# Row-tiled attention masks, and the row maxima sent out from two DMA queues

## Chip, core and metric

The kernel runs on one core of one Trainium2 chip. The metric is the device time in microseconds (us) of one execution. Engines: TensorE (PE; its weight loads PEld), VectorE (DVE), ScalarE (ACT), GpSimd (POOL), and SyncE (SP), which issues most DMAs.

## The reference

A gated block: cross attention of 32 batches (128 queries, 128 keys, 16 heads of 8 dimensions), then a gated mixture of 8 experts on the 4096 tokens.

```
q, k, v = heads(layernorm(x) @ Wq.T + bq), heads(ctx @ Wk.T + bk), heads(ctx @ Wv.T + bv)
scores = einsum('bhqd,bhkd->bhqk', q, k) / sqrt(8)
scores = where(mask[:, None], finfo.min, scores)            # mask: (32, 128, 128) bool
out = merge(softmax(scores) @ v) @ Wo.T + bo
x = x + tanh(g_xattn) * out
w = adapted gate of layernorm(x) over 8 experts, h_e = gelu(y @ W1_e + b1_e)
x = x + tanh(g_ffn) * sum_e w_e * (h_e @ W2_e + b2_e)
```

## The kernel before

**Two phases.** The attention phase walks 16 groups (`g`) of two batches (`b`). Every engine runs `body(it)` for `it` from -6 to 19; `group_at(it, n)` is the group `it + n` if there is one, so that one iteration holds steps of several groups: inputs transposed three ahead, keys and queries (`kq`) two ahead, scores of group `it`, and normalization, Wo and the second layer norm of groups behind. The order of each engine's work is written out by hand, and semaphores tie them. The feed-forward phase (`body_b`) follows, with blocks of 512 tokens; some of its first matmuls are laid into the last attention iterations.

**Scores twice.** `natural(g, b)` makes scores with queries on the partitions: 16 matmuls of 24 rows, four row groups beside each other, into four banks. Then masks are added by matmuls that accumulate: the diagonal matrix `masked_ident` (-2^126) times the mask. Banks 2 and 3 (the low part) come first, banks 0 and 1 (`natural_rest`) later. VectorE takes the negated row maxima out of each pair (`maxima`, L719), splits them into a high and a low part (`max_split`), TensorE transposes the 32 rows (16 high, 16 low; L1147 for b = 0, "max0", and L1215 for b = 1, "max1"), ScalarE copies them to `maxT` (L645, L595), and SP sends them by two DMAs (L415, L407: high parts to row 24 of each row group, low parts to row 25) into `kq_st`. `transposed(g, b)` then makes the scores with keys on the partitions and the maxima taken off (26 rows), with masks again, and ScalarE takes exp (L559) in two halves of two banks. `values` multiplies by v, and `headsT` is copied out, transposed back and normalized to `merged`, which goes through a transpose, a ScalarE copy (`mergedT`, L602) and Wo (L1114).

**Orders that matter here.** On TensorE one iteration is: max1 of the group before, natural(g, 0), transposes of merged and x2n, natural_rest, Wo, values(g-1, 0), kq, transposed(g-1, 1), max0, transposed_rest(g-1, 1), inputs, natural(g, 1), values(g-1, 1), natural_rest(g, 1), v, transposed(g, 0) with its rest, gate, heads. On ScalarE: maxT of max1, exp(g-1, 0, rest), mergedT, x2T, headsT, kq, maxT of max0, exp(g-1, 1, low), exp(g-1, 1, rest), headsT, inputs, exp(g, 0, low). natural(g, 1) waits for exp(g-1, 1, low), since they share banks 2 and 3. On SP: max1's DMAs, then x, ctx, FFN weights and mask (`inputs_ahead`), the four stacks of 192 KB (`stacks`), max0's DMAs, and the stores of kq (`stores`).

**Idle turns** (L972) are matmuls without use at the start, which fill TensorE's waits.

## Time and profile before

| | |
|---|---|
| median of 3 runs | 627.77 us (626.75 to 628.27) |
| profiled execution, whole | 625.05 us |
| its span | 623.2 us |
| busy: PE, DVE, ACT, POOL | 95%, 77%, 61%, 29% |
| instructions | 13765 |

The span runs from the first to the last instruction of the profiled execution. A busy share is an average over both phases. A duration of a matmul in a timeline holds its way through the array, so matmuls overlap; the distance from one start to the next is what it costs.

### The profile page before, as it was taken

The page shows a single profiled execution, that of the slowest core. Times are in us where ns is not written, and L with a number is a line of the kernel's source. Part 1 is how long each engine was busy: PE and PEld are TensorE (multiplying, and loading weights), DVE is VectorE, ACT ScalarE, POOL GpSimd, SP SyncE. Part 2 cuts the span into 40 slices and gives each one's busy share as a digit, 9 for nine tenths or more (in the row PEclk, how much of TensorE's full clock was granted, in tenths as well). Part 3 has the DMA queues.
Part 4 walks back from the last instruction along what each step waited for, and adds up shares of the span by engine and source line. Part 5 has one row for each costly group of instructions (what it writes and reads, how often), then busy time and mean ns, then how long its engine had stood idle before and what let it go on. Part 6 is the DMA issues. An engine that isn't in the chain of part 4 may idle for free.

```text
span 623.2 us, 13765 instructions
## 1 busy us (share of the span) xinstructions
PE 593.8 (95%) x4490; PEld 452.0 (73%) x4490; DVE 479.4 (77%) x940; ACT 378.6 (61%) x625; POOL 178.9 (29%) x224
## 2 busy tenths in 40 slices
PE   7699899999999998999999999999999999999998
PEld 6556566666666655788878788787887887887886
DVE  3457677777776776578879788888888888888886
ACT  2134455555555545767777677677677676776673
POOL 7523344444444221212113212212112112121121
PEclk9969899999999999999999999999999999999999
DMA  6854556555655520041121121111121121111210
GB/s 183 223 150 129 153 160 175 142 141 151 172 150 152 160 64 5 3 102 44 44 68 35 56 68 52 50 57 44 50 67 50 34 67 50 50 61 40 67 51 17
DMA packets 43998, 55.12 MB, mean 88 GB/s; under 512 B 9520, under 2 KB 27824, under 8 KB 42416
## 3 DMA queue, kind: packets, MB, share of 16 engines
q1 hardware_dynamic: 43504, 53.99, 30.5%
q8 instruction: 29, 0.48, 0.3%
q10 hardware_dynamic: 448, 0.53, 0.2%
q14 instruction: 17, 0.14, 0.1%
HBM read 39.16 MB, written 14.81 MB: 87 GB/s over the span
## 4 chain that ended last, share of the span: by engine, by line
PE 82%; DMA 6%; ACT 4%; SPq 4%; DVE 2%; issue 2%; ACTq 0%; DVEq 0%
PE ps_h L1059 10%; PE ps_h L1061 9%; PE ps_h L1060 9%; PE ps_y L1074 9%; PE ps_y L1076 9%; PE ps_y L1075 9%; PE misc L1037 4%; DMA kq_st<-maxT 4%; PE scores L975 4%; PE scores L1003 3%; PE scores L1015 3%; PE scores L992 2%; ACT probs L559 2%; PE misc L1114 1%; DMA kq_scratch<-kq_parts 1%
## 5 line engine op out<-in xcount | busy, mean ns | idle before, releaser
L583 ACT ACTIVATE h_sb<-ps_h,b_sb 128x512 f32<-128x512 f32 x256 | 176.1, 690 | 102.1 <-PE ps_h L1061 92.1
L742 DVE TENSOR_TENSOR h_low<-h_sb,h_high 128x512 fp32r<-128x512 f32 x256 | 164.5, 682 | 0.1
L522 POOL TENSOR_TENSOR yT<-yT,weighted 128x512 f32<-128x512 f32 x54 | 70.9, 1313 | 277.9 <-DVE weighted L917 277.9
L738 DVE CAST h_high<-h_sb 128x512 fp32r<-128x512 f32 x128 | 97.7, 763 | 52.9 <-ACT h_sb L583 52.7
L719 DVE TENSOR_REDUCE neg_max<-scores 128x8 f32<-128x1024 f32 x64 | 77.9, 1221 | 49.1 <-PE scores L975 49.1
L1059 PE MATMUL ps_h<-x_high,w_high 128*128 (+1 forms) x256 | 101.9, 398 | 2.1 <-ACT h_sb L583 2.0
L1074 PE MATMUL ps_y<-h_high,w_high 128*128 128x512 f32 x256 | 100.2, 391 | 0.3 <-ACT h_high L587 0.3
L1061 PE MATMUL ps_h<-x_high,w_low 128*128 (+1 forms) x256 | 99.8, 390 | 0.0
L1076 PE MATMUL ps_y<-h_high,w_low 128*128 128x512 f32 x256 | 99.7, 389 | 0.0
L1060 PE MATMUL ps_h<-x_low,w_high 128*128 (+1 forms) x256 | 99.7, 389 | 0.0
L1075 PE MATMUL ps_y<-h_low,w_high 128*128 128x512 f32 x256 | 99.6, 389 | 0.0
L587 ACT ACTIVATE h_high<-ps_h,b_sb 128x512 fp32r<-128x512 f32 x128 | 87.3, 682 | 0.0
L559 ACT ACTIVATE probs<-scores 128x1024 f32<-128x1024 f32 x64 | 62.9, 1006 | 17.8 <-PE scores L1003 17.8
L1059 PEld LDWEIGHTS ps_h<-x_high,w_high 128*128 128x128 f32 x256 | 48.1, 188 | 14.5 <-issue 4.7
L1074 PEld LDWEIGHTS ps_y<-h_high,w_high 128*128 128x128 f32 x256 | 48.0, 188 | 11.2 <-ACT h_high L587 0.7
L1061 PEld LDWEIGHTS ps_h<-x_high,w_low 128*128 128x128 f32 x256 | 48.1, 188 | 10.3
L1076 PEld LDWEIGHTS ps_y<-h_high,w_low 128*128 128x128 f32 x256 | 48.0, 188 | 10.2
L1075 PEld LDWEIGHTS ps_y<-h_low,w_high 128*128 128x128 f32 x256 | 48.1, 188 | 9.9
L1060 PEld LDWEIGHTS ps_h<-x_low,w_high 128*128 128x128 f32 x256 | 48.1, 188 | 9.3
L917 DVE SCALAR_TENSOR_TENSOR weighted<-ps_y,b_sb,w_row 128x512 f32<-128x512 f32 x55 | 41.0, 745 | 0.0
L975 PE MATMUL scores<-mask_b,masked_ident 128*128 128x512 bf16 x128 | 40.2, 402 | 0.0
L1037 PE MATMUL misc<-probs,v_pad 128*32 128x128 f32 x1024 | 36.3, 285 | 0.3 <-issue 0.3
(127 smaller groups left out, 720.9 us busy)
## 6 DMA issues: line engine op xcount, KB each, us to landing
w_row<-w_scratch SPq DMA_DIRECT2D x64, 256.0 KB, 3.1
kq_st<-kq_scratch SPq DMA_DIRECT2D x64, 192.0 KB
kq_scratch<-kq_parts SPq DMA_DIRECT2D x30, 256.0 KB, 3.2
w_raw<-in_w_ffn SPq DMA_DIRECT2D x16, 256.0 KB, 3.7
kq_scratch<-kq_parts SPq DMA_DIRECT2D x32, 128.0 KB, 3.3
ctx_sb<-in_ctx SPq DMA_DIRECT2D x16, 128.0 KB, 2.6
out_y<-y_out SPq DMA_DIRECT2D x7, 256.0 KB, 2.3
x_all<-in_x SPq DMA_DIRECT2D x13, 128.0 KB, 2.2
```

The lines of the kernel that those rows point to most:

```text
L559: nc.scalar.activation(probs[:, b, half * 8 * S:(half + 1) * 8 * S], scores[:, 2 + 2 * half:4 + 2 * half, :].rearrange("p r x -> p (r x)") ...
L583: nc.scalar.activation(h_sb[:, j % HBUF, :], ps_h[:, j % 4, :], ACT.Gelu_apprx_tanh, bias=b1_sb[:, j:j + 1]).then_inc(h_done, 1)
L587: nc.scalar.activation(h_high[:, j % HBUF, :], ps_h[:, j % 4, :], ACT.Gelu_apprx_tanh, bias=b1_sb[:, j:j + 1]).then_inc(high_even, 1)
L719: nc.vector.tensor_reduce(neg_max[:, b, rows, :], scores[:, rows, :].rearrange("p r (s k) -> p r s k", k=S), AX.X, ALU.max, negate=True).t ...
L738: nc.vector.tensor_copy(h_high[:, j % HBUF, :], h_sb[:, j % HBUF, :]).then_inc(high_odd, 1)
L742: nc.vector.tensor_tensor(h_low[:, j % HBUF, :], h_sb[:, j % HBUF, :], h_high[:, j % HBUF, :].bitcast(F32), ALU.subtract).then_inc(low2_do ...
L1059: mm(dst, w_high[:, e, cols], xh, start=True, stop=False)
L1060: mm(dst, w_high[:, e, cols], xl, start=False, stop=False)
L1061: mm(dst, w_low[:, e, cols], xh, start=False, stop=True).then_inc(h_full, 1)
L1074: mm(dst, w_high[:, E + e, cols], h_high[:, j % HBUF, :], start=(f == 0), stop=False)
L1075: mm(dst, w_high[:, E + e, cols], h_low[:, j % HBUF, :], start=False, stop=False)
L1076: mm(dst, w_low[:, E + e, cols], h_high[:, j % HBUF, :], start=False, stop=(f == FC - 1)).then_inc(w2_done, 1)
```

## The change

Masks: each group's mask is loaded once per batch and repeated for the four row groups (rows 32r to 32r+31 hold queries 4i to 4i+3 in four slices `j`), 128 KB a group instead of 32 KB, by two DMAs, into one buffer instead of two; POOL converts 1024 elements a partition instead of 256. A mask of one pair of banks is 8 matmuls of 32 rows: natural ones of 32x32 with 512 columns, transposed ones of 32x128 with 128 columns. Query columns are dealt out in the order 4i+j when xn is transposed, and put back in the headsT copies. SP: max0's and max1's DMA carries the high parts alone, and the low parts are issued by ScalarE right behind its own copy, ahead of its next exp; masks and ctx stay ahead of the stacks, weights and x move behind max0's DMA, and the six later weights to the end of iteration 0. `merged`, `mergedT` and `x2n` have one buffer instead of two. Three idle turns are new ahead of transposed(0, 0), and six instead of two stand ahead of the first max0.

```diff
-        mask_words = sa("mask_words", [P, 2, GB, S // 4], I32)
-        mask_b = sa("mask_b", [P, 2, GB, S], BF16)
+        mask_words = sa("mask_words", [P, GB, S], I32)
+        mask_b = sa("mask_b", [P, 2, GB, 4, S], BF16)
...
+            def load_mask(g):
+                for b in range(GB):
+                    every = bass.AP(a["mask"].tensor, (g * GB + b) * 32 * S, [[0, ROWS], [S, 32], [1, S]])
+                    sp.dma_start(mask_words[:, b, :], every).then_inc(mask_in[g % 2], 16)
...
+            def masks_and_contexts(it):
+                if (g := group_at(it, 1)) is not None:
+                    if g > 0:
+                        sp.wait_ge(mask_done, g)
+                        load_mask(g)
...
-                    for n in range(2):
-                        sp.dma_start(kq_st[24 + n::32, g % 3, :, 1, 1 * S:(1 + 1) * S].bitcast(F32), maxT[n * H:(n + 1) * H, 1, :].bitcast(F32)).then_inc(max_in[1][g % 3], 16)
+                    sp.dma_start(kq_st[24::32, g % 3, :, 1, 1 * S:(1 + 1) * S].bitcast(F32), maxT[0:H, 1, :].bitcast(F32)).then_inc(max_in[1][g % 3], 16)
                 if it != -1:
-                    inputs_ahead(it)
+                    masks_and_contexts(it)
                 stacks(it)
                 if (g := group_at(it, 0)) is not None:
                     misc_wait_read(sp, "max0", g)
...
+                if it != -1:
+                    weights_and_x(it)
                 stores(it)
                 if it == -1:
-                    inputs_ahead(it)
+                    masks_and_contexts(it)
+                    weights_and_x(it)
+                elif it == 0:
+                    later_weights()
...
                     nc.scalar.activation(maxT[:, 1, :], misc[0:2 * H, bank_of("max1"), 0:S], ACT.Copy).then_inc(misc_read[bank_of("max1")], 1)
+                    misc_wait_read(act, "max1", g)
+                    wait_count(act, tr_low_full, 2 * (g - 3) + 2)
+                    nc.scalar.dma_start(kq_st[25::32, g % 3, :, 1, 1 * S:(1 + 1) * S].bitcast(F32), maxT[H:2 * H, 1, :].bitcast(F32)).then_inc(max_in[1][g % 3], 16)
                     exps(g, 0, 1)
...
-            def natural_mask(r, b, u):
-                return mm(scores[:, r, :].rearrange("p (s k) -> p s k", s=SLABS), masked_ident[:],
-                          mask_b[:, u, b, :].unsqueeze(1).to_broadcast([P, SLABS, S]), start=False, stop=True)
+            def natural_mask(pair, b, u):
+                for j in range(4):
+                    for r in pair:
+                        rows = slice(32 * r, 32 * r + 32)
+                        ins = mm(scores[32 * j:32 * j + 32, r, :].rearrange("p (s k) -> p s k", s=SLABS), masked_ident[rows, rows],
+                                 mask_b[rows, u, b, j, :].unsqueeze(1).to_broadcast([32, SLABS, S]), start=False, stop=True)
+                return ins
...
+            def transposed_mask(pair, b, u):
+                for j in range(4):
+                    for r in pair:
+                        rows = slice(32 * r, 32 * r + 32)
+                        ins = mm(scores[:, 2 + r, :].rearrange("p (s j i) -> p j s i", s=SLABS, j=4)[:, j], mask_b[rows, u, b, j, :],
+                                 masked_ident[rows, rows].unsqueeze(1).to_broadcast([32, SLABS, 32]), start=False, stop=(j == 3))
+                return ins
...
             def transposed(g, b, u):
+                if g == 0 and b == 0:
+                    idle_turns(3)
...
                     if g == 0:
-                        idle_turns(2)
+                        idle_turns(6)
                     pe.wait_ge(max_done[0], g + 1)
```

## Rows read from the trace of the kernel before

**Rows 1.** The page: TensorE's granted clock in tenths, 40 slices.
```profile
PEclk9969899999999999999999999999999999999999
```

**Rows 2.** Timeline of one iteration, TensorE: start us, us, engine, line.
```profile
139.26 0.61 PE L975 MATMUL scores<-mask_b,masked_ident 128*128 128x512 bf16 x2
...
139.70 0.39 PE L966 MATMUL misc<-ident_sb,merged 128*128 128x128 f32 x2
...
140.65 0.68 PE L1114 MATMUL misc<-wo_sb,mergedT 128*128 128x128 f32 x4
...
145.85 0.67 PE L992 MATMUL scores<-kq_st 24*128 24x128 f32 x16 [0.28 <-ACT probs L559]
...
146.45 0.60 PE L975 MATMUL scores<-mask_b,masked_ident 128*128 128x512 bf16 x2
...
146.98 1.08 PE L1037 MATMUL misc<-probs,v_pad 128*32 128x128 f32 x32
...
148.00 0.61 PE L975 MATMUL scores<-mask_b,masked_ident 128*128 128x512 bf16 x2
...
151.11 0.58 PE L1194 MATMUL misc<-wg_sb,x2T_sb 128*128 128x9 f32 x4
```

**Rows 3.** Timeline of the same iteration, the other engines.
```profile
138.73 0.27 ACT L595 ACTIVATE maxT<-misc 32x128 fp32r<-32x128 f32 x1 [0.38 <-PE misc L1215]
...
139.03 1.19 SPq L407 DMA_DIRECT2D kq_st<-maxT  x2
...
140.12 0.39 ACT L602 ACTIVATE mergedT<-misc 128x256 f32<-128x256 f32 x1 [0.22 <-PE misc L966]
...
144.53 0.27 ACT L645 ACTIVATE maxT<-misc 32x128 fp32r<-32x128 f32 x1 [0.40 <-PE misc L1147]
144.71 1.90 ACT L559 ACTIVATE probs<-scores 128x1024 f32<-128x1024 f32 x2
...
147.00 0.40 POOL L505 CAST mask_b<-mask_words 128x256 bf16<-128x256 uint8 x1
...
148.64 1.23 DVE L719 TENSOR_REDUCE neg_max<-scores 128x8 f32<-128x1024 f32 x1 [0.33 <-PE scores L975]
...
150.27 0.70 DVE L853 TENSOR_TENSOR v_pad<-misc,bv_row 128x128 f32<-128x128 f32 x2
```

**Rows 4.** Timeline of ScalarE at the start: its DMA issues and what follows.
```profile
12.69 0.61 ACTq L553 DMA_DIRECT2D kq_scratch<-kq_parts  x1
13.35 0.60 ACT L664 ACTIVATE inT_high<-misc 128x512 fp32r<-128x512 f32 x1 [1.65 <-PE misc L966]
```

**Rows 5.** TensorE's waits from 20 to 250 us: total us, times, longest.
```profile
PE scores L992 <- ACT probs L559: 6.1, 15, 0.9
PE scores L1015 <- DMA kq_st<-maxT: 4.1, 5, 2.5
...
PE misc L966 <- DVE merged L796: 2.0, 3, 1.3
```

**Rows 6.** Timeline at other places: transposes of max0, SP, one wait.
```profile
28.55 0.28 PE L1147 MATMUL misc<-ident_sb,max_parts 128*32 128x128 f32 x1 [2.17 <-DVE max_parts L731]
...
30.07 1.24 SPq L415 DMA_DIRECT2D kq_st<-maxT  x2
...
44.80 0.27 PE L1147 MATMUL misc<-ident_sb,max_parts 128*32 128x128 f32 x1
...
66.09 0.67 PE L1015 MATMUL scores<-kq_st 26*128 26x128 f32 x16 [2.50 <-DMA kq_st<-maxT]
...
239.29 0.28 PE L1147 MATMUL misc<-ident_sb,max_parts 128*32 128x128 f32 x1
```

**Rows 7.** Windows: length, busy us (x) of PE, PEld, DVE, ACT, POOL; PEclk, DMA, GB/s.
```profile
30.00:43.00 13.00, 12.54 (x102) 7.71 (x103) 7.01 (x15) 3.18 (x5) 3.93 (x6) 0.50 0.56 151
...
67.00:71.00 4.00, 4.00 (x29) 2.59 (x28) 0.80 (x3) 2.20 (x3) 1.29 (x2) 0.57 0.02 7
```

**Rows 8.** The page, DMA issues: KB each, median us to landing.
```profile
ctx_sb<-in_ctx SPq DMA_DIRECT2D x16, 128.0 KB, 2.6
```

More of the change, by code:

```diff
@@ L148, in gated_block @@
         sums_r = sa("sums_r", [P, GB * H], F32)
-        merged = sa("merged", [P, 2, GB * H, HD], F32)
-        mergedT = sa("mergedT", [P, 2, GT], F32)
+        merged = sa("merged", [P, GB * H, HD], F32)
+        mergedT = sa("mergedT", [P, GT], F32)
         x_biased = sa("x_biased", [P, GB, D], F32)
@@ L154, in gated_block @@
         rstd2 = sa("rstd2", [P, 2, GB], F32)
-        x2n = sa("x2n", [P, 2, GB, D], F32)
+        x2n = sa("x2n", [P, GB, D], F32)
         x2T = sa("x2T_sb", [P, 2, GT], F32)
@@ L599, in body @@
                     misc_wait_full(act, "merged", g)
-                    if g >= 2:
-                        misc_wait_full(act, "wo", g - 2)
-                    nc.scalar.activation(mergedT[:, u, :], misc[:, bank_of("merged"), 0:GT], ACT.Copy).then_inc(misc_read[bank_of("merged")], 1)
+                    if g >= 1:
+                        misc_wait_full(act, "wo", g - 1)
+                    nc.scalar.activation(mergedT[:], misc[:, bank_of("merged"), 0:GT], ACT.Copy).then_inc(misc_read[bank_of("merged")], 1)
                 if (g := group_at(it, -3)) is not None:
@@ L623, in body @@
                         misc_wait_full(act, "heads", g - 1)
-                    nc.scalar.activation(headsT[:, 0, :], misc[:, bank_of("V0"), 0:2 * P], ACT.Copy).then_inc(misc_read[bank_of("V0")], 1)
+                    nc.scalar.activation(headsT[:, 0, :].rearrange("p (k i j) -> p k j i", k=2, j=4),
+                                         misc[:, bank_of("V0"), 0:2 * P].rearrange("p (k j i) -> p k j i", k=2, j=4), ACT.Copy).then_inc(misc_read[bank_of("V0")], 1)
                     if g == NG - 4:
@@ L645, in body @@
                     nc.scalar.activation(maxT[:, 0, :], misc[0:2 * H, bank_of("max0"), 0:S], ACT.Copy).then_inc(misc_read[bank_of("max0")], 1)
+                    misc_wait_read(act, "max0", g)
+                    wait_count(act, tr_low_full, 2 * (g - 3) + 1)
+                    nc.scalar.dma_start(kq_st[25::32, g % 3, :, 1, 0 * S:(0 + 1) * S].bitcast(F32), maxT[H:2 * H, 0, :].bitcast(F32)).then_inc(max_in[0][g % 3], 16)
                 if (g := group_at(it, -1)) is not None:
@@ L653, in body @@
                         misc_wait_full(act, "heads", g - 1)
-                    nc.scalar.activation(headsT[:, 1, :], misc[:, bank_of("V1"), 0:2 * P], ACT.Copy).then_inc(misc_read[bank_of("V1")], 1)
+                    nc.scalar.activation(headsT[:, 1, :].rearrange("p (k i j) -> p k j i", k=2, j=4),
+                                         misc[:, bank_of("V1"), 0:2 * P].rearrange("p (k j i) -> p k j i", k=2, j=4), ACT.Copy).then_inc(misc_read[bank_of("V1")], 1)
                     if g == NG - 1:
@@ L965, in turn @@
                 for b in range(n):
-                    ins = nc.tensor.transpose(misc[:, k, b * S:(b + 1) * S], src(b), ident[:])
+                    out = misc[:, k, b * S:(b + 1) * S]
+                    ins = nc.tensor.transpose(dealt(out) if b >= GB else out, src(b), ident[:])
                 ins.then_inc(misc_full[k], 1)
```

74 lines of the change are left out of this document (31 added, 43 removed).

## Prediction

> **What bounds the kernel now.** I read the page's slices first [rows 1]: TensorE's granted clock is well below its full level in the third and the fifth slice of 15.6 us and hardly anywhere else. The attention phase ends some 10 us after its last transpose of max0 at 239.29 [rows 6]. The change touches that phase alone; the feed-forward loop keeps its instructions, and I take its time as it is.
>
> The timeline of one iteration [rows 2] comes next, then what the other engines do beside it [rows 3]. An iteration is the path from one transpose of max1 to the next. From max0's transpose at 44.80 to the one at 239.29 lie 14 iterations [rows 6], 13.9 us each. TensorE is busy nearly all of that, but three places are held by others, and they decide what a saved matmul is worth.
> - Wo's matmuls start at 140.65, 0.14 after ScalarE's mergedT ends (140.12 + 0.39) [rows 2, 3].
> - The second natural scores start at 145.85, after 0.28 idle, on ScalarE's exp (the first of the pair of 1.90 that starts at 144.71) [rows 2, 3]. The view of waits puts 6.1 us on this, 15 times [rows 5].
> - The gate's matmuls start at 151.11, 0.14 after VectorE's v_pad ends (150.27 + 0.70). That is late because the second reduce began at 148.64, when the last natural mask was done [rows 2, 3].
>
> The waits for the maxima's DMA are 4.1 us in five places, 2.5 of it in one [rows 5, 6]. The rest of the loss is clock: after 2.17 us of idle before 28.55 the clock is at its half level (1.2 GHz) in 30 to 43, and after the 2.50 us wait before 66.09 again in most of 67 to 71 [rows 6, 7].
>
> **Part 1, ScalarE issues the low maxima: a cost.** A DMA issue occupies ScalarE's sequencer: one took 0.61 from 12.69, and the next activation began at 13.35, 0.05 behind it [rows 4]. For this shape SP needs 1.19 for two, 0.60 each, and starts 0.03 after the copy's end [rows 3]. Behind each of the two new issues an exp is queued that today starts before the copy has even ended.
> - *max1.* Copy ends 139.00 (138.73 + 0.27), issue 139.03 to 139.63, exp 139.68 to 140.68 (two take 1.90 and overlap by 0.1), mergedT 140.58 to 140.97, Wo 141.11: **+0.46** per iteration. Wo exists from iteration 2. In the last three iterations the transpose of merged itself waits for VectorE [rows 5], which covers the delay, so 12 count: +5.5.
> - *max0.* Copy ends 144.80 (144.53 + 0.27), issue 144.83 to 145.43, exp at 145.48 instead of 144.71: **+0.77**, and the second natural scores already wait for it. 14 iterations from the second on: +10.8.
>
> Below, nothing speaks for less than 0.55 an issue (26 x 0.55 = 14.3 without the lost overlap); above, an ACT issue costs the 0.61 + 0.05 seen.
>
> **Part 2, masks in 32-row tiles: a gain.** Today two masks take 0.44 (139.26 to 139.70) [rows 2], so 0.22 for 512 columns. A change of tile shape costs about 0.09: two masks ahead of the 32-column values take 0.53 (146.45 to 146.98) instead of 0.44.
> - *Natural masks* become 8 matmuls of 32x32 with 512 columns, on 2 row groups times 4 column groups. The scores run 16 matmuls on four row groups in 0.60, and the values 32 on four column groups in 1.0 (146.98 to 148.00) [rows 2], 0.13 a round, so either split runs side by side. If both do at once, eight take 0.25 (0.22 as for one mask, and the starts), 0.19 less than now; if only the row groups do, 4 x 0.22 = 0.88. I take 0.25, nearest to what both rows show.
> - *Transposed masks* become 8 matmuls of 128 columns, each with its own weights, on two row groups. Lower bound: 4 turns of 128 columns, 0.22. Upper: rounds like those of the scores (16 in 4 rounds, 0.11 each when the 0.15 for the shape change is off): 0.44, no gain. Their bf16 weight loads are shorter than the scores' fp32, so I take 0.28, 0.16 less.
>
> The Trainium skill speaks on both. *TensorE: Matmul & The Clock Gate* (Packing small matmuls) gives 10.6x for 16 tiles of 32x32, so both splits at once; no row here shows it, and the sum would stand. The same page (LDWEIGHTS) puts a load at its columns over 1.2 GHz, however few its rows: 107 ns for 128, by which the transposed masks would gain nothing; its fast load for non-fp32 would give the lower figure.
>
> What the saving is worth, segment by segment: ahead of Wo nothing, since ScalarE holds it. From Wo to max0 the path is TensorE's: -0.16, 14 times, -2.2. The masks behind max0 stand in the exp's wait: nothing. From the second natural scores to the gate VectorE leads. Its second reduce waits for the values (0.19 earlier, by the low masks) and the rest masks (0.19 shorter, and the shape change ahead of them is there already), so it starts 0.39 sooner and with it v_pad and the gate. TensorE's own path there (low mask -0.19, rest mask hidden by the headsT copy, then about 0.4 saved on the four transposed masks) would be ready 0.25 before. So -0.39, 15 times: -5.9.
>
> Together an iteration grows by 0.46 + 0.77 - 0.16 - 0.39 = 0.68 us.
>
> **Part 3, SP's order and more idle turns: a gain.** max0's DMA today stands behind x, ctx, weights, mask and four stacks. After, one maximum fewer and no x and weights are ahead.
> - The wait before 66.09 should go: -2.5, and -0.9 for the half clock behind it (the clock averages 0.57 from 67 to 71 [rows 7], some 3.4 us at the half level, of which half the cost is hidden by others' work).
> - The other waits for maxima: 4.1 - 2.5 = 1.6 in four places [rows 5], one of them inside the start below, and after the others VectorE is no longer late, so that they cost less than their length: -0.9.
> - *Start.* SP issues max0's DMA at 30.07, 1.5 behind the transpose at 28.55 [rows 6], because six later weights stand ahead of it; the copy between takes 0.27 [rows 3]. The weights now come after it. Four more idle turns (256 columns twice over in two records, so some 0.43 each by the masks' rate, 1.7) fill the 2.17 idle before 28.55, so the clock should hold. 12.54 us of work at half clock in 30 to 43 [rows 7] would need 6.3 less; but the stacks ahead of max0's DMA stay, so its landing moves little, and then ScalarE's chain (two exps, two issues) leads. Walked step by step I get max0 of group 1 at 40.1 instead of 44.80 and the scores behind it, ScalarE's issue included, 3.9 sooner: **-3.9** (bounds: 0 if the clock falls anyway, -5).
>
> **Edits at nothing.** POOL's mask copy has 4 times the elements and took 0.40 [rows 3], so up to 1.6, at 147.00 in its iteration; what it makes is needed at the next one, 5 us on. Single copies of merged, mergedT and x2n wait for reads half an iteration old. The 4-by-32 reordering of xn and headsT has the same number of elements. The load of a mask moves four times the bytes over perhaps fewer DMA engines: two issues instead of one on SP, right behind ctx, some 7 us ahead of POOL's copy, which hides them; with that cover gone, stacks and max0's maxima would slip.
>
> **Sum.** +5.5 + 10.8 - 2.2 - 5.9 - 2.5 - 0.9 - 0.9 - 3.9 = **0.0**. The profiled execution took 625.05 (its span 623.2), 2.7 below the median of 627.77; I put the new median at 627.5.
>
> **Rivals.**
> 1. *ScalarE's issue wins (slower).* If the clock still falls at the start, which gives 0 for -3.9, the loop's +8.2 is set against only 4.3: 631.5. For it: SP's DMA at the start lands behind the same stacks, and TensorE may again idle over 1 us there. It decides as soon as the start gives under 2 us.
> 2. *The issue is partly covered (faster).* If the start gives 5 and a new issue delays its exp by only 0.5, the two terms shrink by 0.27 x 14 and 0.2 x 12, 6.2 in all, and the start adds 1.1: 620.2. Against it stands the 0.66 from 12.69 to 13.35.
> 3. *The half clock enters the loop (slower).* Each iteration gets two idle stretches of 0.7 to 0.9. Today the longest of the 15 waits for the exp, 0.9 [rows 5], came without a fall of the clock, the idle of 2.2 and 2.5 with one [rows 6, 7]. Every fall costs up to 1.7: with four, 634.
> 4. *The 2x4 tiles don't run side by side (slower).* 0.88 for 0.25, for the low and the rest masks of the second natural: +1.2 an iteration, 15 times: 645.
> 5. *Masks clog the DMA engines (slower).* *DMA: Bandwidth & Descriptors* in the Trainium skill (how many engines a copy uses) lets the slowest dimension decide, here 4 for the repeated source: four engines. By itself that leaves the sum alone. By the trace, ctx of the same 128 KB lands in 2.6 [rows 8]; were the masks' transfer to take a multiple of that, the stacks and max0's maxima behind them would slip. Every 0.5 past the slack of an iteration costs 15 x 0.5 = 7.5: 635.
>
> **Chances.** My sum, between -4 and +3: 0.52. Rivals in order: 0.16, 0.20, 0.04, 0.03, 0.05. A measurement of this kernel tells 0.3% (1.9 us) from no change. Of the first case 0.28 falls within that, 0.16 faster and 0.08 slower; rivals 1 and 2 leave 0.02 each within. So faster 0.16 + 0.18 = 0.34, same 0.28 + 0.04 = 0.32, slower 0.08 + 0.14 + 0.12 = 0.34. The range takes the bounds of the start and of the issue: 621 to 634.
>
> **What would show it.** ACTq rows of about 0.6 between maxT's copy and the exp, twice an iteration; the idle before the second natural scores grown from 0.28 to near 0.9; iterations of 14.3; 8 natural masks in 0.25; no half clock between 30 and 43 and none after 66. Wrong if the exp is not delayed by 0.6 or more, if the reduce does not start sooner, or if the half level stays at the start.

## The result and the profile after

The changed kernel takes 681.31 us (median of 4 runs, 674.23 to 691.66), beside 627.26 for the kernel before on the same chip: the ratio is 1.078, with a 95% interval of 1.065 to 1.092. The profiled execution took 674.23. Two of the four runs (687.68 and 691.66) show a further lowered clock, and all ratios here, though not the medians, leave such runs out. The forecast was 627.5 with a range of 621 to 634.

The page of the changed kernel: busy time, the busy share in 40 slices, and the granted clock in the same slices.

```profile
PE 625.8 (93%) x5272; PEld 488.8 (73%) x5272; DVE 480.5 (71%) x940; ACT 390.5 (58%) x625; POOL 189.0 (28%) x224
...
PE   7778998888887889989999999999999999999998
...
PEclk8866557797779775559999999999999999999999
```

[rows 1] had the half level in two places of the start. Here the clock is lowered in all of the first eighteen slices but two, which is nearly the whole attention phase, and full from there on. From the fourth slice on TensorE is busy eight or nine tenths of every slice but one all the same: the busy row alone would have shown nothing.

Measured from one transpose of max0 to the next (the start times in the timeline), the 15 iterations took, with the time at the half level (1.2 GHz) in brackets:

```
before  16.25(13.7) 13.50(0)    17.02(3.4)  13.59(0)    13.71(0)   13.68(0)   14.05(0)
        13.88(0)    13.88(0)    13.66(0)    13.68(0)    13.66(0)   13.67(0)   13.41(0)    13.12(0)
after   14.58(5.7)  19.31(18.2) 20.15(17.1) 18.52(13.7) 16.65(6.8) 16.73(6.8) 14.37(0)
        16.61(6.8)  16.94(6.8)  16.84(6.8)  14.37(0)    16.89(6.8) 16.72(6.8) 19.30(17.1) 18.11(13.7)
```

Two iterations ran wholly at the full level (2.4 GHz): 14.37 each, where the prediction said 14.3. The 49.2 us between the two profiled executions (674.23 - 625.05) split like this: the first max0 comes 1.2 later (29.78 against 28.55), 15 iterations at 14.37 would have been 215.6 against the 210.7 from 28.55 to 239.29, so +4.8; the rest up to 285.86 - 29.78 = 256.1 is **+40.5**, and it stands in iterations with the half level (the first iteration takes about 12 where it has none, as in runs 10 and 12, so the falls cost some 2 more than that); and what follows the last max0 is 2.6 longer. An iteration with 6.8 us at the half level is some 2.4 longer than one without (16.6 to 16.9 against 14.37): 0.35 lost for each microsecond.

Three windows of the changed kernel (columns as in [rows 7]): one iteration and a half at the full clock, the stretch behind it, and what follows.

```profile
134.00:158.00 24.00, 19.76 (x377) 14.86 (x378) 16.45 (x45) 13.60 (x23) 10.53 (x14) 0.99 0.61 159
158.20:164.90 6.70, 6.70 (x76) 4.30 (x73) 4.17 (x11) 2.69 (x6) 3.47 (x6) 0.50 0.41 100
165.00:175.00 10.00, 7.93 (x157) 6.18 (x153) 6.31 (x20) 5.92 (x9) 3.52 (x4) 1.00 0.58 167
```

The clock is full for 24 us in which TensorE idles for 4.2, falls for one stretch in which it is busy throughout, and returns. The view of TensorE's waits from 20 to 310 us (total us, times, longest):

```profile
PE scores L1021 <- ACT probs L570: 18.0, 15, 1.8
PE misc L1213 <- ACT headsT L672: 5.8, 14, 0.5
...
PE scores L1049 <- DMA kq_st<-maxT: 2.0, 3, 1.3
```

[rows 5] had 6.1 us for the first of these, with 0.9 as the longest. The predicted wait is there: 1.07 before the second natural scores, for 0.28 in [rows 2]. Timeline, TensorE, one iteration at the full clock up to 158.2, and the half level from there to 165.0:

```profile
152.51 0.67 PE L1021 MATMUL scores<-kq_st 24*128 24x128 f32 x16 [1.07 <-ACT probs L570]
153.11 0.41 PE L1003 MATMUL scores<-mask_b,masked_ident 32*32 32x512 bf16 x8
153.45 1.08 PE L1069 MATMUL misc<-probs,v_pad 128*32 128x128 f32 x32
...
156.45 0.67 PE L1049 MATMUL scores<-kq_st 26*128 26x128 f32 x16 [0.23 <-DMA kq_st<-maxT]
156.95 0.41 PE L1034 MATMUL scores<-masked_ident,mask_b 32*128 32x128 bf16 x16
157.29 0.61 PE L1226 MATMUL misc<-wg_sb,x2T_sb 128*128 128x9 f32 x4
...
158.73 1.12 PE L1021 MATMUL scores<-kq_st 24*128 24x128 f32 x16
```

and ScalarE beside it, with its own DMA issue (ACTq), then POOL:

```profile
150.40 0.27 ACT L660 ACTIVATE maxT<-misc 32x128 fp32r<-32x128 f32 x1 [0.21 <-PE misc L1179]
150.70 0.54 ACTq L663 DMA_DIRECT2D kq_st<-maxT  x1
151.34 1.94 ACT L570 ACTIVATE probs<-scores 128x1024 f32<-128x1024 f32 x2 [0.67 <-ACT maxT L660]
```

```profile
153.08 1.04 POOL L516 CAST mask_b<-mask_words 128x1024 bf16<-128x1024 uint8 x1
```

The exp starts at 151.34, 0.94 after its maxT copy; in [rows 3] 0.18 after. Eight natural tiles occupy 0.34 up to the values (153.11 to 153.45), the change of shape included, where two masks took 0.53 (146.45 to 146.98 in [rows 2]). The same 16 matmuls of 24 rows show 0.67 at the full level (152.51) and 1.12 at the half level (158.73): that is how the clock is read off a timeline.

The start, which was to be 3.9 sooner:

```profile
29.78 0.27 PE L1179 MATMUL misc<-ident_sb,max_parts 128*32 128x128 f32 x1
...
35.52 0.67 PE L1049 MATMUL scores<-kq_st 26*128 26x128 f32 x16 [1.27 <-DMA kq_st<-maxT]
...
37.63 0.67 PE L1021 MATMUL scores<-kq_st 24*128 24x128 f32 x16 [0.99 <-ACT probs L570]
...
39.42 1.93 PE L1069 MATMUL misc<-probs,v_pad 128*32 128x128 f32 x32 [0.76 <-ACT probs L570]
```

Waits of 1.27 and 0.99 end within 2.1 us, the clock goes to the half level at 38.7, as a third wait of 0.76 begins, and it stays there for 24 us. The values at 39.42 show 1.93 instead of 1.08. The second max0 comes at 29.78 + 14.58 = 44.36, 0.4 sooner than the 44.80 of before, where the prediction had 40.1.

### The profile page after: what moved, and what is told of

Read it like the earlier page. It is cut to its first block, busy times and chain, and to the rows that moved or that the text cites. A ratio compares the mean times of both kernels' runs of the same rounds, so it can differ in the third digit from the quotient of the medians.

```text
span 672.4 us, 15374 instructions
## 1 busy us (share of the span) xinstructions
PE 625.8 (93%) x5272; PEld 488.8 (73%) x5272; DVE 480.5 (71%) x940; ACT 390.5 (58%) x625; POOL 189.0 (28%) x224
## 4 chain that ended last, share of the span: by engine, by line
PE 76%; ACT 5%; issue 2%; DMA 2%; DVE 1%; ACTq 1%; POOL 0%; DVEq 0%
PE ps_h L1091 9%; PE ps_h L1093 9%; PE ps_h L1092 8%; PE ps_y L1106 8%; PE ps_y L1107 8%; PE ps_y L1108 8%; PE misc L1069 6%; PE scores L1021 3%; PE scores L1003 3%; PE misc L1146 2%; PE scores L1049 2%; PE misc L990 2%; DMA kq_st<-maxT 2%; ACT probs L570 2%; PE misc L1226 1%
## 5 line engine op out<-in xcount | busy, mean ns | idle before, releaser
L1069 PE MATMUL misc<-probs,v_pad 128*32 128x128 f32 x1024 | 50.7, 362 | 1.2 <-ACT probs L570 0.8
L1021 PE MATMUL scores<-kq_st 24*128 24x128 f32 x512 | 28.9, 355 | 21.7 <-ACT probs L570 18.0
L1021 PEld LDWEIGHTS scores<-kq_st 24*128 24x128 f32 x512 | 24.2, 253 | 29.6 <-issue 26.2
```

The source lines that it names most:

```text
L1069: ins = mm(misc[32 * t:32 * t + 32, k_bank, k * P:(k + 1) * P], v_pad[:, u, b, h, :], probs[:, b, at:at + S], start=(o == 0), stop=(o == 1))
```

## The experiments

Iteration times are those of the profiled execution, again from max0 to max0. "At the full clock" is the length of those with nothing at the half level. Two executions were profiled of the kernels of runs 1 to 4: the lines shown are of the first (spans 658.0, 641.9, 661.8 and 688.7), the iteration times and the time at the half level of the second (663.1, 639.9, 646.7 and 684.0).

**1. Both DMAs of a maximum on SP, tiled masks kept.** Is it ScalarE's issue?

```diff
-                    nc.scalar.dma_start(kq_st[25::32, ...], maxT[H:2 * H, 0, :]...)      # and for max1
+                    sp.dma_start(kq_st[25::32, ...], maxT[H:2 * H, 0, :]...)             # behind the high part's
```

> The changed kernel with both DMAs of each row maximum back on SP; tiled masks, SP's order and idle turns stay. Theory A (TensorE idles 1.07 before the second natural scores and some 0.5 before Wo, because ScalarE issues DMAs, and that idle is what takes the clock down): the two idle stretches shrink by about 0.6 and 0.7 each, the half level is gone from the loop, and the time is 615 to 622, under the kernel before. Theory B (the masks in small tiles load the array less, and that takes the clock down): the half level stays in the loop, at least 60 us of it, and the time is above 650. If both are needed: in between, some iterations at half clock, 630 to 650.

Measured: 660.44, ratio 1.055 (1.047 to 1.062). Five iterations of 13.0 to 13.2 are at the full clock; the other ten take 14.2 to 19.9, with 4.7 to 19.2 at the half level. Waits of TensorE:

```profile
PE scores L1045 <- DMA kq_st<-maxT: 13.8, 7, 2.5
PE scores L1017 <- ACT probs L572: 6.9, 16, 1.0
```

The waits for exp are back where they were in [rows 5], and seven waits for a maximum's DMA have come. ScalarE's issue accounts for 14.37 - 13.1 = 1.27 of an iteration at the full clock. The falls don't need it; whether the new waits bring them here is left to run 11.

**2. 128-row masks in the old layout, with SP's order, ScalarE's issues and the idle turns of the change.** What goes with the tiles is as before too: the 32 KB mask load, the order of the queries and with it headsT's plain copy, and two copies of merged and x2n.

```diff
-                natural_mask((2, 3), b, u).then_inc(nat_low_full, 1)
+                natural_mask(2, b, u)
+                natural_mask(3, b, u).then_inc(nat_low_full, 1)     # one 128x128, 512 columns, a bank
```

> The kernel before with everything of the change but the tiled masks and what goes with them (128-row masks, one mask load a group, no dealt order, two copies of merged and x2n): SP's order, the low maxima issued by ScalarE, the idle turns. Theory A (ScalarE's issues make the idle that takes the clock down): the half level shows in the loop as in the changed kernel, time 665 or more. Theory B (small tiles take it down): the loop stays at the full level; an iteration is 13.7 + 0.46 + 0.77 = 14.9 at most, and with the gains at the start the time is 632 to 640. If both are needed: a few falls, 640 to 660.

Measured: 641.99, ratio 1.021 (1.013 to 1.028). Iterations of some 14.93 at the full clock, and only two with 3.4 at the half level. Waits, then windows:

```profile
PE scores L1004 <- ACT probs L565: 19.2, 17, 1.7
```

```profile
120.00:140.00 20.00, 18.39 (x247) 12.35 (x247) 15.13 (x40) 9.70 (x17) 6.38 (x10) 1.00 0.57 165
...
160.00:180.00 20.00, 17.37 (x229) 11.28 (x231) 12.72 (x39) 10.74 (x19) 9.72 (x15) 1.00 0.57 154
```

TensorE waits as often and as long for the exp as in the changed kernel (17 times, up to 1.7), and is busy 17.4 to 18.4 of 20 us, at the full clock. In the changed kernel 24 us with 19.8 busy ended in a fall. The waits for the exp alone, then, don't bring the falls: something on the masks' side has a part in it, and this run can't tell the tiles from the larger load, the slower copy or a smaller busy share.

**3. Seven idle matmuls (fp32r, 256 columns) in the wait before the second natural scores**, else the changed kernel.

```diff
+                if b == 1 and g > 0:
+                    filler(7)
                 pe.wait_ge(kq_in[g % 3], g // 3 * 64 + 64)
```

> The changed kernel with 7 idle matmuls of 256 columns (128x128 weights, some 0.8 us at the full clock) laid into the wait before the second natural scores of each group from the second on, written to a bank that is overwritten next. Both theories say that more work in the wait keeps the clock up if the clock is what costs: iterations of 14.4 throughout and a time of 622 to 632, since the matmuls stand where TensorE waits anyway. If the clock falls for another reason than what TensorE does in a stretch, the time stays at 670 or more.

Measured: 659.25, ratio 1.052 (1.046 to 1.058). The wait for exp shrank to 3.7 us in 9 places, yet 9 of 15 iterations still have 6.8 at the half level. Filling the largest wait helps by some 15 us and does not cure it: 659 lies between the two cases that were expected (622 to 632, or 670 and more).

**4. headsT's copy reads with the stride and writes in one piece.** The changed copy writes every fourth element. The tile's rows, changed kernel, then this one (min/median/max in ns):

```profile
L638 ACT ACTIVATE headsT<-misc x16: 622/636/650, 41.4 to 301.5; 128x256 f32<-128x256 f32 x16
L672 ACT ACTIVATE headsT<-misc x16: 604/618/621, 50.5 to 305.7; 128x256 f32<-128x256 f32 x16
```

```profile
L638 ACT ACTIVATE headsT<-misc x16: 384/384/386, 42.1 to 317.6; 128x256 f32<-128x256 f32 x16
```

```diff
-                    nc.scalar.activation(headsT[:, 0, :].rearrange("p (k i j) -> p k j i", k=2, j=4),
-                                         misc[...].rearrange("p (k j i) -> p k j i", k=2, j=4), ACT.Copy)
+                    nc.scalar.activation(headsT[:, 0, :].rearrange("p (k i j) -> p k i j", k=2, j=4),
+                                         misc[...].rearrange("p (k j i) -> p k i j", k=2, j=4), ACT.Copy)
```

> The changed kernel with the headsT copies reading with a stride and writing contiguously, where the changed kernel writes with a stride of four elements. The copy took 0.38 before and 0.62 after. If the strided write is what costs: the copy takes 0.4 again, TensorE's wait for it before v (5.8 us in all) mostly goes, and the clock, being near its limit, falls less often: 650 to 672. If any reordering costs: 0.6 again and no change, 674 to 682.

Measured: the copy takes 0.384 again, and the kernel 688.94, ratio 1.099 (1.093 to 1.106), outside both expected ranges, with 189 us at the half level instead of 155. A part became faster by 0.24 and the whole was slower. Why is not shown, only that the time went with the falls and not with the length of the step.

**5. Natural masks back at 128 rows**, transposed tiles kept (one of the four slices serves for all queries here and in the next: in this input a batch's mask is the same for every query, so a general kernel would need a second layout).

```diff
-                for j in range(4):
-                    for r in pair:
-                        rows = slice(32 * r, 32 * r + 32)
-                        ins = mm(scores[32 * j:32 * j + 32, r, :]..., masked_ident[rows, rows], mask_b[rows, u, b, j, :]...)
+                for r in pair:
+                    ins = mm(scores[:, r, :]..., masked_ident[:], mask_b[:, u, b, 0, :]...)
```

> The changed kernel with only the natural masks back to matmuls of 128 rows and columns (two of 512 columns a pair; they take one slice of the mask, so they add the mask of other queries); transposed masks stay in 32-row tiles. An iteration at the full clock should be 14.4 + 0.2. If the 32x32 tiles are what loads the array too little: nearly no fall in the loop, time 630 to 640. If the transposed tiles are: falls as in the changed kernel, 665 or more. If only the sum of both counts: about half the falls, 645 to 660.

**6. Transposed masks back at 128 rows**, natural tiles kept.

```diff
-                                 mask_b[rows, u, b, j, :], masked_ident[rows, rows].unsqueeze(1).to_broadcast([32, SLABS, 32])
+                                 mask_b[:, u, b, 0, :], masked_ident[:].unsqueeze(1).to_broadcast([P, SLABS, S])   # no loop over j
```

> The changed kernel with only the transposed masks back to matmuls of 128 rows (they take one slice of the mask, so they add the mask of other queries); natural masks stay 32x32. If the transposed tiles are what loads the array too little: nearly no fall in the loop and 630 to 640. If the 32x32 tiles are: falls as in the changed kernel, 665 or more. If only the sum of both counts: about half the falls, 645 to 660.

Measured: 671.59, ratio 1.074 (1.068 to 1.080) for the first; 653.05, ratio 1.041 (1.031 to 1.050) for the second. The granted clock of the two, in this order:

```profile
PEclk8887788888777778779999999999999999999999
```

```profile
PEclk9869999999999595689999999999999999999999
```

With transposed tiles alone nine of the 15 iterations are 17.1 with 6.8 at the half level, and none is without a fall. With natural tiles alone they are 14.2 to 15.3 at the full clock, but for four (the first two, and two of the last three). The falls come with the transposed tiles in the main. But 653 is in the range expected for "only the sum of both counts" (645 to 660) and not in 630 to 640, so something else has a part; runs 9 and 12 find it in the mask loads.

The timeline of this second kernel also gives the tiles' own price:

```profile
121.33 0.67 PE L1021 MATMUL scores<-kq_st 24*128 24x128 f32 x16 [1.07 <-ACT probs L570]
...
125.40 0.67 PE L1047 MATMUL scores<-kq_st 26*128 26x128 f32 x16 [0.36 <-DMA kq_st<-maxT]
...
126.87 0.51 PE L1224 MATMUL misc<-wg_sb,x2T_sb 128*128 128x9 f32 x4
```

From the second transposed scores to the gate it takes 1.47 (125.40 to 126.87); with the tiles 0.84 (156.45 to 157.29). Eight tiles save 0.32, not the 0.16 of the prediction. And the kernel of run 6 shows that it is not the busy share that decides:

```profile
60.00:200.00 140.00, 118.37 (x1901) 82.01 (x1899) 99.63 (x262) 77.28 (x132) 67.25 (x95) 1.00 0.63 157
```

TensorE is busy 85% of these 140 us, little more than the 82% of the changed kernel ahead of its fall, and the clock holds throughout.

**7. The kernel before with SP's order, the later weights at iteration 0's end, and the idle turns**; old masks, SP issues both parts.

```diff
                 if it != -1:
-                    inputs_ahead(it)
+                    masks_and_contexts(it)       # the old 32 KB mask, then ctx
                 stacks(it)
...                                               # max0's two DMAs
+                if it != -1:
+                    weights_and_x(it)
```

> The kernel before with only SP's order (mask and ctx, stacks, maxima, then weights, x and stores), the six later weights after iteration 0, and the idle turns; both DMAs of a maximum on SP, old masks. By the terms of my sum: start 4 to 5 sooner (the kernel with old masks and ScalarE's issues had 12.07 for the first iteration instead of 16.25), the wait of 2.5 with its half clock gone, other maxima's waits mostly gone: 616 to 620, faster than before. If SP's order brings nothing by itself: 621 to 627.

Measured: **620.68**, ratio 0.993 (0.989 to 0.997). Against run 2, which differs by ScalarE's issues alone, an iteration is 13.68 instead of 14.93: the issues cost 1.25. The second max0 comes at 28.03 + 12.79 = 40.8 instead of 44.8, 4.0 sooner. The next iteration gives it all back (17.90 instead of 13.50):

```profile
48.30 1.12 PE L1025 MATMUL scores<-kq_st 26*128 26x128 f32 x16 [2.19 <-DMA kq_st<-maxT]
```

TensorE is ready 2.2 ahead of the maxima, and the clock is at the half level from 47.4 on, for 6.8.

**8. Every transposed mask tile issued twice.**

```diff
-                for j in range(4):
+                for n in range(8):
+                    j = n % 4
...
-                                 masked_ident[rows, rows]...
+                                 (masked_ident if n < 4 else ident_b)[rows, rows]...
```

> The changed kernel with every transposed mask put out twice, 16 matmuls of 32x128 with 128 columns instead of 8 (the second time with the plain identity, which adds 1 to -2^126 and changes nothing). 8 of them took about 0.17 in the timeline of the changed kernel, so the four masks of an iteration grow by about 0.7 and take nearly what the four pairs of 128-row matmuls took before (0.44 each). Theory A, the short time that the masks now take is what lets the clock fall (less matmul work between the waits): with that work given back the clock stays up as in the run with the transposed masks at 128 rows (half clock in two iterations, 653), the iteration is 15.0 and the time 640 to 658. Theory B, these matmuls of 32 rows are themselves what the clock goes down with, however many there are: the iterations keep 6.8 or more at half clock, 17 or longer, and the time is 680 to 695.

Measured: 686.67, ratio 1.103 (1.097 to 1.109). Timeline and clock:

```profile
121.41 0.39 PE L1035 MATMUL scores<-masked_ident,mask_b 32*128 32x128 bf16 x8
121.65 0.38 PE L1035 MATMUL scores<-ident_b,mask_b 32*128 32x128 bf16 x8
121.96 0.28 PE L1180 MATMUL misc<-ident_sb,max_parts 128*32 128x128 f32 x1
```

```profile
PEclk9965597588777777558999999999999999999999
```

The masks now take 0.55 up to the transpose of max0 (121.41 to 121.96), as long as the 0.53 of two masks with a change of shape behind them in [rows 2], and the falls are as many (162 us at the half level). That the masks had become short is not the reason.

**9. Both DMAs on SP, natural tiles, transposed masks at 128 rows:** the edits of runs 1 and 6 together.

> The changed kernel with both DMAs of a maximum on SP and the transposed masks back at 128 rows; natural masks of 32x32 tiles, the larger mask load and SP's new order stay. If the falls of the clock come with the transposed tiles, the loop is at full clock nearly throughout, and an iteration is that of the run with the transposed masks at 128 rows (14.7) without ScalarE's issues (1.25 measured as the difference of two pairs of runs): 13.4, time 612 to 622, faster than the kernel before. Rival: the larger mask loads delay SP's maxima, as where both were on SP and both masks tiled (waits of up to 2.5 for the DMA of maxT, 7 times), and each such wait brings a fall to half clock: 625 to 645, slower than the version with SP's order alone (620.7).

Measured: 653.38, ratio 1.048 (1.043 to 1.052), slower than even the rival's 625 to 645. Nine iterations of 13.2 to 15.0 at the full clock alternate with six of 16.1 to 20.4. Waits:

```profile
PE scores L1043 <- DMA kq_st<-maxT: 15.7, 10, 2.9
```

The maxima are late: from the end of SP's issue to the last landing max0's took 4.4 (median of 16), against 1.2 for max1's and 3.0 for max0's in the kernel before.

**10. Run 7 with four idle turns where it waits 2.2.**

```diff
+                if g == 1 and b == 0:
+                    pe.wait_ge(nat_low_read, 2 * g + 2)
+                    wait_count(pe, tr_low_read, 2 * g + b)
+                    wait_count(pe, tr_rest_read, 2 * g + b)
+                    idle_turns(4)
                 pe.wait_ge(max_in[b][g % 3], g // 3 * 32 + 32)
```

> The kernel before with SP's new order and the idle turns of the change (128-row masks, SP issues both maxima; 620.7), and four more idle turns where TensorE waits 2.2 for the maxima of the second group's first batch, at 46 to 48. Theory: the half clock from 47.4 on, 6.8 us of it, is set off by that wait; with the wait filled it is gone and the time falls by 2 to 3, to 617.5 to 619. Rival: the fall comes anyway (the turns end before the wait does, or the load at the start brings it), and the time stays at 620 to 621.5.

Measured: **618.84**, ratio 0.990 (0.987 to 0.993). Timeline, the turns and the scores behind them:

```profile
45.62 1.94 PE L980 MATMUL scores<-x2T_sb 128*128 128x256 f32 x8
48.13 0.67 PE L1030 MATMUL scores<-kq_st 26*128 26x128 f32 x16 [0.57 <-DMA kq_st<-maxT]
```

The scores start 0.2 earlier than in run 7 and at the full clock (0.67, not 1.12). No iteration has a microsecond at the half level, and the second one is 15.61 instead of 17.90. The trace shows the fall gone; the 1.8 us between the two medians are within the intervals of both ratios.

**11 to 13. The mask loaded for the first group alone** (the other 15 groups get its mask, so their results are wrong), in three kernels: run 1 (all masks tiled, SP issues), run 9 (natural ones alone), and the changed kernel.

```diff
                 if (g := group_at(it, 1)) is not None:
                     if g > 0:
-                        sp.wait_ge(mask_done, g)
-                        load_mask(g)
+                        pass
```

> The changed kernel with both DMAs of a maximum on SP and both masks tiled (first experiment), but the mask is loaded for the first group alone and its words are used for all 16, so the masks of the other groups are wrong and 30 of the 32 mask loads are left out. Theory A, the larger mask loads make SP's maxima late (7 waits of up to 2.5 for the DMA of maxT) and these waits set off the clock's falls: without the loads the waits go, every iteration is 13.1 at full clock, and the time is 608 to 616. Theory B, the transposed 32-row tiles take the clock down with small waits too: the waits for maxT go, but falls of 3.4 to 10 per iteration stay in most of them, and the time is 630 to 655.

> The changed kernel with both DMAs of a maximum on SP, transposed masks at 128 rows, natural ones of 32x32 tiles (653.4 with all loads, 10 waits for the DMA of maxT of up to 2.9), and the mask loaded for the first group alone (the other groups' masks are wrong). If the loads are what makes the maxima late, the 10 waits go, iterations are 13.4 at full clock throughout, and the time is 612 to 618, below the 620.7 of SP's order alone. Rival: the waits come from SP's new order or from the larger natural share and stay at 2 or more: 640 to 655.

> The changed kernel, nothing undone, with the mask loaded for the first group alone (the other groups' masks are wrong). Its waits for a DMA of maxT were only 3 in the loop, so if the falls come of the transposed tiles together with the 15 waits of up to 1.8 for the exp that ScalarE's issue delays, nothing changes: iterations of 16.7 with 6.8 at half clock, 670 to 685. Rival: the four times larger loads have a part in it by another way (they delay kq or the stacks); then the falls thin out and the time is 625 to 655.

Measured: 645.78, ratio 1.032 (1.024 to 1.040) for all masks tiled; 615.15, ratio 0.988 (0.983 to 0.994) for natural ones alone; the changed kernel 663.12 in the one run that counts, with 6.8 to 17 at the half level in 11 of 15 iterations, between the two ranges expected. Clock and waits of the first (its profiled run, 656.76, is one that the ratio leaves out, but the three others, with a mean granted clock of 0.915 to 0.928, have the falls too; 1 is the full level, and run 12's has 0.986 to 0.994):

```profile
PEclk9786589788889565679999999999999999999999
```

```profile
PE scores L1018 <- ACT probs L573: 6.4, 15, 1.0
...
PE scores L1018 <- DMA kq_st<-kq_scratch: 2.9, 1, 2.9
```

and of the second:

```profile
PEclk8899999999999999999999999999999999999999
```

```profile
PE scores L1018 <- ACT probs L573: 7.0, 17, 0.9
...
PE scores L1018 <- DMA kq_st<-kq_scratch: 2.5, 1, 2.5
```

Windows, the first two of run 11, each just ahead of a fall, the third of run 12:

```profile
92.80:116.40 23.60, 21.48 (x420) 15.97 (x408) 18.57 (x54) 14.46 (x25) 10.99 (x17) 1.00 0.57 161
123.40:143.70 20.30, 18.20 (x368) 13.47 (x365) 15.11 (x37) 12.28 (x22) 9.76 (x13) 1.00 0.53 148
```

```profile
80.00:220.00 140.00, 129.48 (x2101) 90.63 (x2101) 108.18 (x283) 82.92 (x146) 67.81 (x94) 1.00 0.55 153
```

This is the cleanest pair: the two kernels differ by the transposed masks alone. The waits are alike (for exp 15 and 17 times, none above 1.0; one for the stacks at the start, 2.9 and 2.5; for a maximum's DMA one of 1.6 and two of at most 1.3). One has the transposed masks as tiles and 3.4 or more at the half level in 11 of its 15 iterations; the other has them at 128 rows and not one. The busy share doesn't tell them apart: 90% and 91% ahead of two falls in run 11, 92% without one in run 12, and 85% without one in run 6. The pair of runs 9 and 12 shows what made the maxima late in run 9: without the loads max0's landed in 1.7 instead of 4.4, and 38 us are gone.

The changed kernel loses by the loads too, at its start: in run 13 the first four iterations take 59.1 together, in the changed kernel 72.6, and the eleven behind them 183.7 and 183.5 (one execution of each).

**14 and 15. The loads put elsewhere on SP's queue**, for the group two ahead, in run 9 with the four turns of run 10: behind max0's DMAs, and at the end of SP's iteration.

```diff
-                if (g := group_at(it, 1)) is not None:           # behind max1's DMAs, ahead of ctx
-                    if g > 0:
-                        sp.wait_ge(mask_done, g)
-                        load_mask(g)
+                if (g := group_at(it, 2)) is not None and g > 0: # behind max0's DMAs; 15: behind the stores
+                    sp.wait_ge(mask_done, g)
+                    load_mask(g)
```

> Both DMAs of a maximum on SP, natural masks of 32x32 tiles, transposed masks at 128 rows (each takes one of the four slices, which serves because the mask of a batch is here the same for every query), four idle turns before the second transposed scores, and the mask loads moved: for the group two ahead, right behind max0's DMAs, instead of for the group one ahead behind max1's and ahead of ctx and the stacks. Theory, the loads delayed the maxima only because they stood ahead of them: the 10 waits of up to 2.9 go, iterations are 13.4 at full clock, 612 to 617, as without the loads (615.2) or a little better for the turns. Rival: the transfer of 128 KB delays a maximum or the stores of kq wherever it stands, waits of 1 to 3 stay and bring falls: 625 to 655.

> The same kernel with the mask loads at the end of SP's iteration, behind the stores of kq and some 3 ahead of max1's DMAs. If a load issued about 3 before a maximum still holds it up, max1 is now the late one and the time is 625 to 655; if 3 are enough, 612 to 617, as with the loads behind max0.

Measured: 625.02, ratio 1.000 (0.996 to 1.004), and **618.28**, ratio 0.992 (0.988 to 0.996). Of the ten waits three are left, and one. Run 14's row:

```profile
PE scores L1047 <- DMA kq_st<-maxT: 3.1, 3, 2.4
```

All but three and two iterations are 13.1 to 13.6. The place did it: at the end of SP's iteration max0's maxima land in 1.8 (median). The profiled execution of run 15 is the slowest of its ten (625.79, the others 616.86 to 624.27): at its start TensorE waits 3.8 once, and the third max0 comes at 66.4, against 56.1 in run 10. How much of that is in the faster ones, whose median is just above the 612 to 617 expected, isn't shown.

**16. Short matmuls with all rows:** the transposed masks as 8 matmuls of 128 columns with a load each, but 128 rows.

```diff
-                                 mask_b[rows, u, b, j, :], masked_ident[rows, rows].unsqueeze(1).to_broadcast([32, SLABS, 32])
+                                 mask_b[:, u, b, 0, :], masked_ident[:, 32 * j:32 * j + 32].unsqueeze(1).to_broadcast([P, SLABS, 32])
```

> The changed kernel with the transposed masks in as many and as short matmuls as the tiles (8 for a pair of banks, 128 columns each, a weight load for each), but with all 128 rows of the array instead of 32 (each takes one of the four slices, which serves because the mask of a batch is here the same for every query). They run one behind the other, so 8 take about the 0.43 of two masks of 512 columns. Theory A, it is the 32 rows that bring the falls of the clock: with full rows the loop stays at full clock as in the run with the transposed masks at 128 rows (14.7 an iteration), 645 to 660. Theory B, it is the many short matmuls with their loads: falls of 6.8 in most iterations stay, 675 to 695.

Measured: ratio 1.047 (1.038 to 1.056); the two runs that count took 652.4 and 656.8, the others 669.5 and 676.3. Timeline, 8 masks up to the transpose of max0:

```profile
159.35 0.62 PE L1033 MATMUL scores<-masked_ident,mask_b 128*128 128x128 bf16 x8
159.80 0.27 PE L1178 MATMUL misc<-ident_sb,max_parts 128*32 128x128 f32 x1
```

Within their intervals this is run 6 (1.031 to 1.050), not the changed kernel (1.065 to 1.092). So most of it goes with the 32 rows, and not with the matmuls being short, nor with the order in which they write their columns, which is that of the tiles. In the profiled execution, one of the two others, 7 iterations keep falls of 6.8 or more; a part for the shortness is therefore not excluded.

## Why the prediction was wrong

**The step that failed** is rival 3, the half clock in the loop, at 0.04, and under it the unspoken term of every sum: that the clock in the loop stays what it was. The prediction judged the clock by idle stretches alone ("the longest of the 15 waits for the exp, 0.9, came without a fall") and never asked what the new matmul shapes do to it. Run 2 has waits for the exp of up to 1.7 and hardly a fall; runs 11 and 12 have the same waits of at most 1.0 for it, and only the one with 32-row transposed tiles falls in the loop. A fall of 6.8 cost 2.4 where 1.7 was said, but the number of falls is the error: four were priced, and 13 of 15 iterations had time at the half level, +40.5 in the loop. And where rival 3 has the two idle stretches as the cause, run 11 keeps the falls without ScalarE's issues: the cause shown is the transposed tiles.

What held:
- **ScalarE's issue.** Predicted 0.46 + 0.77 = 1.23 an iteration; measured 1.25 (run 2 against 7) and 1.27 (run 1 against the changed kernel). The issue itself took 0.54, with 0.67 of idle before the exp. The prediction charged it in 12 and 14 of the iterations, 16.3 in all; run 2 is some 17 slower than run 7 by their ratios.
- **The masks.** Predicted -0.16 - 0.39 = -0.55; measured 13.68 to 13.1, -0.58 (run 7 against 1), with the slower headsT copy and the larger load in it. The split was off: natural tiles bring 0.28 (13.68 to 13.4, run 7 against 12, the copy in it), transposed ones 0.3 (run 12 against 1), since 8 of those save 0.32 and not 0.16.
- **The rule on weight loads** that would have denied that gain does not set the pace here. The Trainium skill (*TensorE: Matmul & The Clock Gate*, LDWEIGHTS) has columns over 1.2 GHz, 107 ns for 128, so four loads in turn on a row group would take 0.43, an estimate by that page. One load of a tile did take 93 (median of 512, row below), but 16 matmuls with their loads pass in 0.34 (156.95 to 157.29), four row groups side by side: rounds of four start at 157.02, 157.07 and 157.13. The same page's fast load for weights that aren't fp32 (Weight-path perf modes, about twice as fast, so an estimate of 53 ns) fits these rounds; whether the load or the matmul sets them isn't shown.

```profile
L1034 PEld LDWEIGHTS scores<-masked_ident,mask_b x512: 90/93/147, 36.0 to 302.1; 32*128 32x128 bf16 x171
```

- **The iteration.** 14.3 predicted, 14.37 measured at the full clock, in the two that had it.
- **The wait before 66.09** is gone: in runs 7 and 10 the third iteration takes 13.6 instead of 17.02.

What was mis-sized beside that:
- **SP's order and the idle turns** (part 3) were put at 8.2 together. Run 7, which has them alone, gives 4.4 (620.68 against 625.06 of the kernel before on its chip). Of the start's 3.9, run 7 shows 4.0 at the second max0 and loses it in the next iteration to a wait of 2.2 and a half clock of 6.8 behind it; in the changed kernel it is 0.4, with a half clock of 24 us behind it. That was rival 1's condition, the start under 2, and it explains little of the 50.
- **headsT's copy** was put at nothing ("the same number of elements") and went from 0.385 to 0.62 and 0.64, with a new wait of up to 0.5 behind it 14 times.
- **The mask load** was also put at nothing, and rival 5 at 0.05. In the changed kernel three waits for maxT, 2.0 us in all, are what the view of waits shows of it, but without the loads the first four iterations take 13.4 less (run 13, one execution). In the shorter iterations of run 9 it costs 38 us (against run 12): POOL is served in time, and it is max0's maxima, behind mask, ctx and stacks, that are late, as rival 5 had it. So part of the 40.5 is the loads', by waits or falls at the start; the falls of the other eleven iterations stay without them.

**What stays open.** Why 32-row transposed tiles go with a lower clock, and not the natural ones of 32x32, is not settled. Both keep two of the four row groups at work; the natural ones run 512 columns and the transposed ones 128 with 128-column weights. Transposed masks of 32 rows with 512 columns would tell, and weren't tried.

## What to carry to other kernels

Price a change twice: once at the clock of before, and once for what it does to the granted clock, and count a new matmul shape in the second even where it only saves time. Read the length of an iteration at the full clock apart from the time at the half level; here the iteration at the full clock was forecast to 0.1 us and the total was wrong by over 50. A transfer that grows belongs behind the short urgent ones on its queue (runs 9, 14 and 15), and filling an idle stretch of 2 us early in this kernel kept the clock up: SP's order with seven new idle turns and four more (run 10) gives 618.84, ratio 0.990, with no mask touched.

## What the runs showed of the hardware

- Eight tiles of 32x128 with 128 bf16 columns on two row groups, in place of two of 128x128 with 512, came with 6.8 us or more at the half clock in most iterations (runs 5, 8, 11), at waits and a busy share that had none without them (run 12, 92% busy; run 6, 85%). Issued twice: the same. Tiles of 32x32 with 512 columns: none (run 12).
- TensorE at the half level is as busy as ever: 6.70 of 6.70 us in the window from 158.20. Only the granted clock and the durations (0.67 to 1.12) tell.
- A ScalarE copy of 128x256 fp32 that writes every fourth element takes 0.62 to 0.64, one that reads so 0.384, as one in order (0.385 before).
- 128 KB of mask from a source repeated four times landed 3.0 us (median) after SP's second issue. max0's maxima, 16 KB, took 4.4 behind mask, ctx and stacks, and 1.7 behind ctx and stacks alone (runs 9 and 12).
